# Twelve of 39 expert blocks transposed by DMA from 16-bit planes, in a fused linear and mixture-of-experts kernel

## The chip, the cores and the metric

The kernel runs on one core of one Trainium2 chip. The metric is device time in microseconds (us); lower is better. TensorE (PE) multiplies, ScalarE (ACT), VectorE (DVE) and GpSimd (POOL) do the elementwise work, SyncE (SP) issues most DMAs; POOL issues the indirect ones.

## The reference

2048 tokens of width 1024 pass a linear layer whose weight is masked in 32x32 blocks, and then a mixture of eight experts of which each token takes two:

```python
w_masked = weight * elem_mask
x = x + layernorm(x) @ w_masked.T            # x: 2048 x 1024
z = layernorm(x)
logits = z @ W_gate + b_gate
top_idx = top_k(logits, 2)
y_all = relu(z @ W_e[e] + b_e[e])            # e = 0..7, W_e[e]: 1024 x 1024
x = x + mean(y_all[top_idx])
```

All is fp32. A product is done as three passes of fp32r matmuls: high part by high part, high by low, low by high, so each operand is split into a rounded half (HI) and a rest (LO).

## The kernel before, in words

**Projection, about 0 to 220 us.** 16 token blocks of 128. For block t, PE multiplies x (xT) with the masked weight (wT) in two column halves of three passes of eight matmuls (`project_pass(t, n, pass)`). ACT first writes a row scaled by the block's mean into the PSUM half (`seed_mean(t, n)`, from t = 4 on; PE's first pass of a half waits for it through `c_sown`). `x_hi(t)` (ACT) and `x_lo(t)` (DVE) split the block's input; `mean1`, `square1` sum its rows; `residual`, `stats2` (DVE) and `inverse_std2` (POOL) give the second layer norm, and ACT's `norm2(t)` writes the normed rows into x2, a ring of two, from where SP stores them to DRAM (`store_x2`, tensor x2_rows). The gate's products go `gate(t)` (PE), `gate_out(t)` (ACT, copies them to gated), `logits(t)` (PE, waits for `gate_out(t)`). On PE the order around t = 4 is: pass (3,1,2), logits(0), gate(1), pass (4,0,0), logits(1), gate(2), passes (4,0,1) and (4,0,2), gate(3), logits(2), pass (4,1,0), gate(4). Up to t = 8 the order of each engine is written out by hand; a loop writes the rest. In the loop ACT also makes the HI half of the first expert's eight weight chunks (`HI0_AT`).

**Experts, about 220 to 690 us.** 39 blocks b of 128 rows, each of one expert. POOL gathers the block's rows by token number from x2_rows (`gather_rows`, ring of four buffers), PE transposes them (`transpose_rows`: eight 128x128 transposes against an identity, into PSUM) at the start of block b-1, ACT copies the result twice (`rows_hi`: xT HI, then x2T in fp32; both count in `c_rhi`), POOL subtracts to LO (`rows_lo`). PE then does two halves of 24 matmuls. ACT writes the bias into PSUM ahead of each half (`seed_half`), takes the relu of it into xb after it, and POOL adds xb to the output by an indirect DMA (`add_rows`). DVE splits the next expert's eight weight chunks (`split_chunk`) as soon as the expert that used the slot is through.

Every engine works in its own written order; semaphores tie them. An instruction that waits holds all behind it on its engine. ACT's order in block b is: rows of b+1, relu of half 0, bias of half 0 of b+1, relu of half 1, bias of half 1 of b+1.

Of the kernel before, what the change touches and what calls it, by code (L numbers as in the profile page):

```python
# [9 lines left out]
I32 = mybir.dt.int32  # L10
ALU = mybir.AluOpType
# [3 lines left out]
P = 128  # L15
# [7 lines left out]
def build(nc, data, weight, w_gate, b_gate, w_e, b_e, data_t, weight_t, mask_blocks, out):  # L23
# [26 lines left out]
    with ctx:  # L50

        x2_rows = nc.dram_tensor("x2_rows", (N_TOK, D), F32, kind="Internal").ap()

# [25 lines left out]

        raw = sb("raw", [P, 2, H], F32)  # L80
        bias_slot = sb("bias_slot", [P, 2, H], F32)
# [116 lines left out]
        through = sb("through", [P, N_EXP], I32)  # L198
        tok_half = sb("tok_half", [P, NH], I32)
        assert cursor[0] <= xr_offset + 2 * D * 4 and end <= nc.sbuf_usable_end  # L200

        def rows_of(b, cols=slice(0, D)):
            return (rows_a[:, cols], rows_b[:, cols], x2[:, 0, cols], x2[:, 1, cols])[b % 4]
# [90 lines left out]
        c_first, c_pick = sem("c_first"), sem("c_pick")  # L294
        c_tok_half = sem("c_tok_half")
# [4 lines left out]
        HI0_AT = {10: (0,), 11: (1, 2), 12: (3, 4), 13: (5, 6), 14: (7,)}  # L300
        GATHER_AT = NB - 2

# [18 lines left out]
        def _(eng):  # L321
# [71 lines left out]
            for t in (1, 2):  # L393
                store_x1(t)
                store_x2(t)
# [11 lines left out]
            for i in range(FIRST, NB + 1):  # L407
                if FIRST + 3 <= i + 1 < NB:
                    load_rows(i + 1)
                store_x1(i - 1)  # L410
# [9 lines left out]
                store_x2(i - 1)  # L420

            eng.wait_ge(s_spare, 16)
# [20 lines left out]
        def _(eng):  # L443
# [284 lines left out]
            def transpose_rows(b):  # L728
                eng.wait_ge(l_gather[b % 4], 16 * (b // 4 + 1))
# [68 lines left out]
            for b in range(EARLY, N_BLOCKS):  # L798
                if b > EARLY and b + 1 < N_BLOCKS:
# [3 lines left out]
                eng.wait_ge(c_rhi, 2 * b - 1)  # L803
# [15 lines left out]
        def _(eng):  # L819
# [75 lines left out]

            def norm2(t):
                if t >= 2:
                    eng.wait_ge(l_x2[t % 2], 16 * (t // 2))
                eng.wait_ge(c_rs2, RS2 * (t + 1))
# [27 lines left out]
            x_hi(2)  # L927
            mean1(1)
            square1(1)
            sum_diagonal(0)  # L930
            sum_diagonal(1)
            x_hi(3)
            sum_diagonal(2)
            sum_diagonal(3)
            sum_diagonal(4)
            mean1(2)
            square1(2)
            sum_diagonal(5)
            mean1(3)
# [774 lines left out]
```

## Time and profile before

| | us |
|---|---|
| median of 3 runs | 692.05 (690.92 to 694.01) |
| the profiled execution | 691.73 |
| its span | 689.5 |
| PE busy, share of the span | 671.3, 97% |
| DVE, ACT, POOL busy | 307.7, 289.5, 282.6 |
| granted TensorE clock, mean | 0.994 of full |

The span runs from the first to the last instruction on the engines. A busy PE is not PE at its peak: the ends of matmuls are modelled, and where instructions follow each other closely what counts is the distance between their starts. The expert stage is 39 blocks of about 11.8 us.

### The profile page before, as it was taken

The page shows a single profiled execution, that of the slowest core. Times are in us where ns is not written, and L with a number is a line of the kernel's source. Part 1 is how long each engine was busy: PE and PEld are TensorE (multiplying, and loading weights), DVE is VectorE, ACT ScalarE, POOL GpSimd, SP SyncE. Part 2 cuts the span into 40 slices and gives each one's busy share as a digit, 9 for nine tenths or more (in the row PEclk, how much of TensorE's full clock was granted, in tenths as well). Part 3 has the DMA queues.
Part 4 walks back from the last instruction along what each step waited for, and adds up shares of the span by engine and source line. Part 5 has one row for each costly group of instructions (what it writes and reads, how often), then busy time and mean ns, then how long its engine had stood idle before and what let it go on. Part 6 is the DMA issues. An engine that isn't in the chain of part 4 may idle for free.

```text
span 689.5 us, 11082 instructions
## 1 busy us (share of the span) xinstructions
PE 671.3 (97%) x3551; PEld 547.0 (79%) x3551; DVE 307.7 (45%) x551; ACT 289.5 (42%) x421; POOL 282.6 (41%) x253
## 2 busy tenths in 40 slices
PE   6999999999999999999999999999999999999993
PEld 5667777888887888888888888888888888888883
DVE  5886688877985562460642610551533420000000
ACT  7875544455743343333334343434333333434330
POOL 2023122135661365363635444463535363534331
PEclk9999999999999999999999999999999999999997
DMA  8992735497552579594784855694875854322223
GB/s 350 407 397 65 279 118 189 165 323 259 188 202 85 184 196 257 163 245 123 203 254 97 251 150 115 171 241 109 236 221 112 257 113 95 53 44 43 49 35 57
DMA packets 34900, 122.39 MB, mean 177 GB/s; under 512 B 5024, under 2 KB 5024, under 8 KB 34848
## 3 DMA queue, kind: packets, MB, share of 16 engines
q1 hardware_dynamic: 23472, 84.46, 33.7%
q0 software_dynamic: 11376, 37.23, 26.4%
q8 instruction: 33, 0.54, 0.3%
q14 instruction: 19, 0.16, 0.1%
HBM read 87.59 MB, written 37.75 MB: 182 GB/s over the span
## 4 chain that ended last, share of the span: by engine, by line
PE 96%; DMA 1%; ACT 1%; issue 0%; SPq 0%; POOLq 0%; DVE 0%; ACTq 0%
PE psO L449 83%; PE psT L739 5%; PE psT L449 2%; PE psT L482 2%; PE psO L482 1%; PE psG L555 1%; DMA xb<-data_t 1%; PE psS L536 1%; PE psT L523 0%; PE psT L567 0%; POOLq L50 0%; PE psT L544 0%; DVE w_stage L1318 0%; SPq L347 0%; ACT xT L829 0%
## 5 line engine op out<-in xcount | busy, mean ns | idle before, releaser
L449 PE MATMUL psO<-slots,xT 128*128 (+1 forms) x1872 | 435.9, 392 | 0.0
L449 PEld LDWEIGHTS psO<-slots,xT 128*128 128x128 f32 x1872 | 348.2, 188 | 70.6
L1056 ACT ACTIVATE xb<-psO 128x512 f32<-128x512 f32 x78 | 46.7, 599 | 254.5 <-PE psO L449 254.5
L449 PE MATMUL psO<-wT,xT 128*128 128x512 f32 x624 | 152.3, 397 | 0.8 <-ACT psO L887 0.8
L1645 POOL DMA_INDIRECT rows_out<-xb,tok_of x36 | 61.4, 1704 | 212.1 <-ACT xb L1056 211.8
L1306 DVE CAST slots<-raw 128x1024 fp32r<-128x1024 f32 x56 | 49.7, 887 | 191.0 <-PE psO L449 108.8
L449 PEld LDWEIGHTS psO<-wT,xT 128*128 128x128 f32 x624 | 114.3, 188 | 25.9 <-issue 2.7
L1639 POOL TENSOR_TENSOR xT<-x2T,xT 128x1024 fp32r<-128x1024 f32 x38 | 98.0, 2579 | 18.0 <-ACT x2T L1035 17.8
L1308 DVE TENSOR_TENSOR slots<-raw,slots 128x1024 fp32r<-128x1024 f32 x56 | 81.3, 1452 | 1.9
L996 ACT ACTIVATE psO<-bias_slot 128x512 f32 (+1 forms) x78 | 47.0, 602 | 35.6 <-ACT xb L1056 19.6
L1030 ACT ACTIVATE xT<-psT 128x1024 fp32r<-128x1024 f32 x38 | 38.4, 1011 | 7.5 <-PE psT L739 7.5
L1035 ACT ACTIVATE x2T<-psT 128x1024 f32<-128x1024 f32 x38 | 38.7, 1017 | 0.0
L1578 POOL TENSOR_SCALAR rs<-squares 128x1 f32<-128x1 f32 x16 | 9.5, 594 | 69.5 <-ACT rows_a L863 41.1
L1591 POOL TENSOR_SCALAR rs<-mv 128x1 f32<-128x1 f32 x16 | 5.2, 328 | 66.2 <-DVE mv L1097 66.1
L1604 POOL DMA_INDIRECT x<-x_rows,tok_of x19 | 25.5, 1344 | 6.1 <-DVE tok_of L1504 3.1
L829 ACT ACTIVATE xT<-xb 128x1024 fp32r<-128x1024 f32 x12 | 12.7, 1061 | 25.0 <-PE psO L449 19.4
L1631 POOL TENSOR_TENSOR slots<-w_stage,slots 128x1024 fp32r<-128x1024 f32 x8 | 19.2, 2416 | 9.5 <-ACT slots L1016 9.5
L739 PEld LDWEIGHTS psT<-ident,x 128*128 128x128 f32 x152 | 17.7, 140 | 2.5
L739 PE MATMUL psT<-ident,x 128*128 128x128 f32 x152 | 19.7, 272 | 0.0
L1165 DVE TENSOR_TENSOR row_hot<-lane,pos_r 128x1024 f16<-128x1024 f16 x16 | 19.5, 1217 | 0.0
L887 ACT ACTIVATE psO<-raw,minus_mean 128x512 f32<-128x512 f32 x24 | 16.3, 679 | 5.7 <-DVE xr L1110 4.3
L482 PE MATMUL psO<-wT,xT 128*128 128x512 f32 x48 | 13.5, 402 | 3.1 <-ACT wT L843 3.1
(227 smaller groups left out, 507.5 us busy)
## 6 DMA issues: line engine op xcount, KB each, us to landing
raw<-L_ffn_W_e SPq DMA_DIRECT2D x56, 512.0 KB, 5.1
x_rows<-x SPq DMA_DIRECT2D x16, 512.0 KB, 4.6
xb<-data_t SPq DMA_DIRECT2D x12, 512.0 KB, 4.3
mask_stage<-mask_blocks SPq DMA_DIRECT2D x8, 512.0 KB, 10.5
w_stage<-weight_t SPq DMA_DIRECT2D x8, 512.0 KB, 11.2
row_stage<-L_attn_weight SPq DMA_DIRECT2D x8, 512.0 KB, 12.2
xr<-L_attn_data SPq DMA_DIRECT2D x8, 512.0 KB, 5.7
rows_out<-xr SPq DMA_DIRECT2D x8, 512.0 KB, 3.0
```

The costliest lines, as they stand in the source:

```text
L449: last = eng.matmul(psum, xT[:, p, a, kt, :], moving(b, kt), start=(i == 0 and kt == 0 and not seeded), stop=(i == len(PASSES) - 1 and kt ...
L482: mm = eng.matmul(acc(t, n), xT[:, t, part_x, c, :], wT[:, part_w, c, n * HALF:(n + 1) * HALF], start=(i == 0 and c == 0), stop=(i == 1 an ...
L739: last = eng.transpose(psT[:, turn_bank(b), kt, :], rows_of(b, slice(kt * P, (kt + 1) * P)), ident[:])
L996: eng.activation(psO[:, n, :], bias, ACT.Copy).then_inc(c_seed, 1)
L1030: eng.activation(xT[:, b % 2, HI, :, :], psT[:, turn_bank(b), :, :], ACT.Copy).then_inc(c_rhi, 1)
L1035: eng.activation(x2T[:], psT[:, turn_bank(b), :, :], ACT.Copy).then_inc(c_rhi, 1)
L1056: eng.activation(xb[:, b % 2, n * HALF:(n + 1) * HALF], psO[:, n, :], ACT.Relu, scale=1.0 / TOP_K).then_inc(c_out, 1)
L1306: eng.tensor_copy(slots[:, e % 2, HI, kt, :], raw[:, kt % 2, :]).then_inc(c_split, 1)
L1308: eng.tensor_tensor(slots[:, e % 2, LO, kt, :], raw[:, kt % 2, :], slots[:, e % 2, HI, kt, :].bitcast(F32), ALU.subtract).then_inc(c_split, 1)
L1604: eng.indirect_dma_start(rows_of(b), None, x2_rows[0:known, :], bass.IndirectOffsetOnAxis(ap=tok_col(b), axis=0), bounds_check=known - 1, ...
L1639: eng.tensor_tensor(xT[:, b % 2, LO, :, :], x2T[:], xT[:, b % 2, HI, :, :].bitcast(F32), ALU.subtract).then_inc(c_rlo, 1)
L1645: eng.indirect_dma_start(out, bass.IndirectOffsetOnAxis(ap=tok_col(b), axis=0), xb[:, b % 2, :], None, bounds_check=N_TOK + P - 1, compute ...
```

## The change

Twelve blocks (b = 5, 8, 11, ..., 38) are no longer transposed by PE. For this the normed rows are also stored as two planes of 16-bit halves: ACT copies each 128x1024 fp32 block as 128x2048 16-bit values into `planes` (a single buffer, over raw[0]), SP stores it to a second DRAM tensor. For those twelve blocks POOL gathers plane rows into x2[1], a DMA issued by ACT transposes them into `turned`, and ACT joins the halves into x2T and rounds that to xT. The other blocks share three row buffers. In the written-out part of the projection ACT's order is new; one HI chunk of the first expert comes up to one iteration later; SP waits for the last planes store ahead of the second expert's weights, which land in the same buffer; and DVE's chunk splits for experts 2 to 7 are released in pairs, half a block apart, in place of all at once.

```diff
+        planes = at("planes", [P, 2, D], U16, raw_offset)
+        turned = at("turned", [P, 2 * KT, P], U16, xr_offset + D * 4)
         def rows_of(b, cols=slice(0, D)):
-            return (rows_a[:, cols], rows_b[:, cols], x2[:, 0, cols], x2[:, 1, cols])[b % 4]
+            ring = 3 if by_dma(b) else turns_of_pe(b) % 3
+            return (rows_a[:, cols], rows_b[:, cols], x2[:, 0, cols], x2[:, 1, cols])[ring]
-        HI0_AT = {10: (0,), 11: (1, 2), 12: (3, 4), 13: (5, 6), 14: (7,)}
+        HI0_AT = {10: (0,), 11: (1, 2), 12: (3,), 13: (4, 5), 14: (6,), 15: (7,)}
+        def by_dma(b):
+            return b > EARLY + 2 and b % 3 == 2
...
+            def store_planes(t):
+                eng.wait_ge(c_planes, t + 1)
+                eng.dma_start(x2_planes[t * P:(t + 1) * P, :], planes[:].rearrange("p h d -> p (h d)")).then_inc(l_planes, 16)
             store_x2(0)
             load_x(7)
-            for t in (1, 2):
-                store_x1(t)
-                store_x2(t)
+            store_planes(0)
+            store_x1(1)
+            store_x2(1)
+            store_planes(1)
+            store_x1(2)
+            store_x2(2)
...
+                store_planes(i - 2)
                 store_x1(i - 1)
...
-            eng.wait_ge(s_spare, 16)
+            eng.wait_ge(l_planes, 16 * NB)
...
-                if b > EARLY and b + 1 < N_BLOCKS:
+                if b > EARLY and b + 1 < N_BLOCKS and not by_dma(b + 1):
                     transpose_rows(b + 1)
-                eng.wait_ge(c_rhi, 2 * b - 1)
+                eng.wait_ge(c_rhi, 2 * b if by_dma(b) else 2 * b - 1)
...
+            def split_planes(t):
+                eng.wait_ge(c_ln2, t + 1)
+                if t == 0:
+                    eng.wait_ge(s_spare, 16)
+                else:
+                    eng.wait_ge(l_planes, 16 * t)
+                eng.activation(planes[:], x2[:, t % 2, :].bitcast(U16).rearrange("p (d h) -> p h d", h=2), ACT.Copy).then_inc(c_planes, 1)
...
+            norm2(0)
+            split_planes(0)
             gate_out(0)
-            norm2(0)
+            x_hi(5)
+            norm2(1)
             seed_mean(4, 0)
+            split_planes(1)
             gate_out(1)
-            x_hi(5)
             seed_mean(4, 1)
             gate_out(2)
...
+            def turn_rows(b):
+                eng.wait_ge(l_gather[3], 16 * turns_of_dma(b))
...
+                eng.dma_start_transpose(turned[:], rows_of(b).bitcast(U16)).then_inc(l_turn, 16)
+            def join_rows(b):
+                eng.wait_ge(l_turn, 16 * turns_of_dma(b))
+                eng.wait_ge(c_rlo, b - 1)
+                eng.activation(x2T[:].bitcast(U16).rearrange("p k (t h) -> p h (k t)", h=2),
+                               turned[:].rearrange("p (h k) t -> p h (k t)", h=2), ACT.Copy).then_inc(c_rhi, 1)
+                eng.wait_ge(c_rhi, 2 * b - 1)
+                eng.wait_ge(c_half, NH * b)
+                eng.activation(xT[:, b % 2, HI, :, :], x2T[:], ACT.Copy).then_inc(c_rhi, 1)
...
+                if b + 1 < N_BLOCKS and by_dma(b + 1):
+                    join_rows(b + 1)
...
+                    if n == NH - 1 and b + 3 < N_BLOCKS and by_dma(b + 3):
+                        turn_rows(b + 3)
...
             for e in range(2, N_EXP):
                 for kt in range(KT):
+                    if kt % 2 == 0:
+                        when = pace[0:1, kt // 2 - 1, e - 2:e - 1] if kt > 0 else through[0:1, e - 2:e - 1]
+                        used = eng.value_load(when, min_val=NH, max_val=NH * (N_BLOCKS + 1))
+                        eng.wait_ge(c_half, used)
                     split_chunk(e, kt)
...
+            eng.wait_ge(c_planes, NB)
+            eng.memset(x2[:, 1, :], 0.0).then_inc(c_clear, 1)
             add_rows(0)
             for b in range(1, N_BLOCKS):
-                if b + 1 < N_BLOCKS:
+                if b + 1 < N_BLOCKS and not by_dma(b + 1):
                     rows_lo(b + 1)
-                if b + 3 < N_BLOCKS:
+                if b + 3 < N_BLOCKS and not by_dma(b + 3):
                     gather_rows(b + 3)
+                if b + 4 < N_BLOCKS and by_dma(b + 4):
+                    gather_rows(b + 4)
+                if b + 1 < N_BLOCKS and by_dma(b + 1):
+                    rows_lo(b + 1)
```

**ACT in the written-out part of the projection, before.** From `square1(5)` on; psT,squares is `square1`, gated is `gate_out`, x2 is `norm2`, psO is `seed_mean`, xT is `x_hi`.

```order
L863 ACTIVATE psT,squares1_103<-xr_58,minus_mean1_102 128x1024
L894 ACTIVATE gated_82<-psG 128x128
L900 ACTIVATE x2_60<-w_stage_50,shift2_99,inverse2_98 128x1024
L887 ACTIVATE psO<-raw_55,minus_mean1_102 128x512
L894 ACTIVATE gated_82<-psG 128x128
L829 ACTIVATE xT_59<-w_stage_50 128x1024
L887 ACTIVATE psO<-raw_55,minus_mean1_102 128x512
```

**The same place on ACT, changed.** The new name planes is `split_planes`.

```order
L890 ACTIVATE psT,squares1_104<-xr_59,minus_mean1_103 128x1024
L936 ACTIVATE x2_61<-w_stage_50,shift2_100,inverse2_99 128x1024
L929 ACTIVATE planes_56<-x2_61 128x2048
L921 ACTIVATE gated_83<-psG 128x128
L856 ACTIVATE xT_60<-w_stage_50 128x1024
L936 ACTIVATE x2_61<-w_stage_50,shift2_100,inverse2_99 128x1024
L914 ACTIVATE psO<-raw_55,minus_mean1_103 128x512
L929 ACTIVATE planes_56<-x2_61 128x2048
L921 ACTIVATE gated_83<-psG 128x128
L914 ACTIVATE psO<-raw_55,minus_mean1_103 128x512
```

`x_hi(5)` and `norm2(1)` now stand ahead of `seed_mean(4, 0)`, and the planes copies of blocks 0 and 1 ahead of `gate_out(0)` and `gate_out(1)`.

**SP at the same time, before.** rows_out<-w_stage is `store_x1`, x_rows `store_x2`, xb<-data_t `load_x(7)`.

```order
L358 DMA rows_out<-w_stage 128x1024
L362 DMA x_rows<-x_60 128x1024
L332 DMA xb<-data_t 128x1024
L358 DMA rows_out<-w_stage 128x1024
L362 DMA x_rows<-x_60 128x1024
```

**The same place on SP, changed.**

```order
L376 DMA rows_out<-w_stage 128x1024
L380 DMA x_rows<-x_61 128x1024
L350 DMA xb<-data_t 128x1024
L384 DMA x_planes<-planes 128x2048
L376 DMA rows_out<-w_stage 128x1024
L380 DMA x_rows<-x_61 128x1024
L384 DMA x_planes<-planes 128x2048
```

The store of the planes of block 0 stands behind `load_x(7)`, and that of block 1 behind `store_x2(1)`.

**ACT in the expert stage, before, in one block.** xb<-psO is the relu, psO<-bias_slot the bias of the next block, xT and x2T are `rows_hi`.

```order
L1056 ACTIVATE xb_57<-psO 128x512
L996 ISA
L996 ACTIVATE psO<-bias_slot_56 128x512
L1030 ACTIVATE xT_59<-psT 128x1024
L1035 ACTIVATE x2T_61<-psT 128x1024
L1056 ACTIVATE xb_57<-psO 128x512
```

**ACT in the expert stage, changed: the end of block 2, and the rows of block 5 in block 4.** turned is the DMA's destination; the first piece stands behind block 2's last bias, the second ahead of block 4's first relu.

```order
L1123 ACTIVATE xb_58<-psO 128x512
L1039 ISA
L1039 ACTIVATE psO<-bias_slot_57 128x512
L1077 DMA_TRANSPOSE turned_165<-x2_61 128x16x128
L1095 ACTIVATE xT_60<-psT 128x1024
...
L1039 ACTIVATE psO<-bias_slot_57 128x512
L1082 ACTIVATE x2T_62<-turned_165 128x2x1024
L1086 ACTIVATE xT_60<-x2T_62 128x1024
L1123 ACTIVATE xb_58<-psO 128x512
```

The DMA for block b+3 is issued at the end of ACT's part of block b, one block and a piece ahead of the copy that reads it.

## Rows read from the trace of the kernel before

**Rows 1.** The page, part 4: the chain that ended last, by engine.

```profile
PE 96%; DMA 1%; ACT 1%; issue 0%; SPq 0%; POOLq 0%; DVE 0%; ACTq 0%
```

**Rows 2.** PE's waits, whole span: waited for, us in total, times, longest.

```profile
PE psO L449 <- ACT psO L887: 0.8, 1, 0.8
```

**Rows 3.** Timeline of PE, expert stage: start us, us, engine, line.

```profile
255.64 1.04 PE L739 MATMUL psT<-ident,rows_a 128*128 128x128 f32 x8
...
645.26 11.18 PE L449 MATMUL psO<-slots,xT 128*128 x48
656.28 1.03 PE L739 MATMUL psT<-ident,x 128*128 128x128 f32 x8
657.07 22.03 PE L449 MATMUL psO<-slots,xT 128*128 x96
```

**Rows 4.** Timeline of PE and ACT over one block, 409 to 428 us.

```profile
409.73 0.60 ACT L996 ACTIVATE psO<-bias_slot 128x512 f32 x1
...
421.40 11.16 PE L449 MATMUL psO<-slots,xT 128*128 x48
421.54 0.60 ACT L996 ACTIVATE psO<-bias_slot 128x512 f32 x1
...
427.21 0.60 ACT L1056 ACTIVATE xb<-psO 128x512 f32<-128x512 f32 x1 [3.21 <-PE psO L449]
```

**Rows 5.** The page, part 5: busy us, mean ns of one, idle before.

```profile
L996 ACT ACTIVATE psO<-bias_slot 128x512 f32 (+1 forms) x78 | 47.0, 602 | 35.6 <-ACT xb L1056 19.6
L829 ACT ACTIVATE xT<-xb 128x1024 fp32r<-128x1024 f32 x12 | 12.7, 1061 | 25.0 <-PE psO L449 19.4
```

**Rows 6.** DMA issues, 380 to 430 us: median us from issue to landing.

```profile
rows_out<-xb,tok_of POOLq DMA_INDIRECT x4, 6.4
x<-x_rows,tok_of POOLq DMA_INDIRECT x2, 4.8
```

**Rows 7.** Timeline of the written-out projection, 64 to 77 us.

```profile
64.48 2.12 PE L449 MATMUL psO<-wT,xT 128*128 128x512 f32 x8
64.79 1.23 ACT L900 ACTIVATE x<-w_stage,shift,inverse 128x1024 f32<-128x1024 f32 x1
65.78 0.27 POOL L1596 TENSOR_SCALAR shift<-mv,inverse 128x1 f32<-128x1 f32 x1
65.92 0.68 ACT L887 ACTIVATE psO<-raw,minus_mean 128x512 f32<-128x512 f32 x1
...
67.22 2.12 PE L449 MATMUL psO<-wT,xT 128*128 128x512 f32 x8
67.36 0.28 ACT L894 ACTIVATE gated<-psG 128x128 f32<-128x128 f32 x1 [0.76 <-PE psG L555]
67.40 0.33 SPq L332 DMA_DIRECT2D xb<-data_t  x1
...
69.18 0.29 PE L567 MATMUL psT<-diagonal,gated 128*128 128x16 f32 x2
...
76.68 0.64 PE L555 MATMUL psG<-w_stage,gates 128*32 128x128 f32 x16
```

**Rows 8.** DMA issues, 60 to 90 us: KB, median us to landing.

```profile
rows_out<-w_stage SPq DMA_DIRECT2D x4, 512.0 KB, 5.5
```

**Rows 9.** Line L362, the 16 stores of x2.

```profile
DMA to landing us min/median/max: 2.6/4.6/7.4
```

**Rows 10.** Timeline, 118 to 120 us: ACT's seed of block 8, PE's use.

```profile
118.47 0.67 ACT L887 ACTIVATE psO<-raw,minus_mean 128x512 f32<-128x512 f32 x1
119.70 5.71 PE L449 MATMUL psO<-wT,xT 128*128 128x512 f32 x24
```

**Rows 11.** One-us window behind PE's last matmul: busy times, then PEclk, DMA.

```profile
681.00:682.00 1.00, 0.00 (x0) 0.00 (x0) 0.00 (x0) 0.00 (x0) 0.63 (x1) 0.77 0.00 0
```

**Rows 12.** Timeline of DVE: end of one expert's splits, start of the next.

```profile
306.57 3.29 DVE L1308 TENSOR_TENSOR slots<-raw,slots 128x1024 fp32r<-128x1024 f32 x1
326.54 0.69 DVE L1306 CAST slots<-raw 128x1024 fp32r<-128x1024 f32 x1 [16.68 <-PE psO L449]
```

More of the change, by code:

```diff
@@ L10 @@
 I32 = mybir.dt.int32
+U16 = mybir.dt.uint16
 ALU = mybir.AluOpType
@@ L299, in build, with turns_of_pe, turns_of_dma @@
         FIRST_KNOWN, FIRST_TOK = 4, 15
-        HI0_AT = {10: (0,), 11: (1, 2), 12: (3, 4), 13: (5, 6), 14: (7,)}
+        HI0_AT = {10: (0,), 11: (1, 2), 12: (3,), 13: (4, 5), 14: (6,), 15: (7,)}
         GATHER_AT = NB - 2
+        def by_dma(b):
+            return b > EARLY + 2 and b % 3 == 2
+        def turns_of_pe(b):
+            return len([c for c in range(1, b + 1) if not by_dma(c)])
+        def turns_of_dma(b):
+            return len([c for c in range(1, b + 1) if by_dma(c)])
         def turn_bank(b):
@@ L949, in _ @@
             square1(5)
+            norm2(0)
+            split_planes(0)
             gate_out(0)
-            norm2(0)
+            x_hi(5)
+            norm2(1)
             seed_mean(4, 0)
+            split_planes(1)
             gate_out(1)
-            x_hi(5)
             seed_mean(4, 1)
             gate_out(2)
-            norm2(1)
-            mean1(6)
+            norm2(2)
+            split_planes(2)
+            norm2(3)
             gate_out(3)
             seed_mean(5, 0)
+            split_planes(3)
+            gate_out(4)
+            mean1(6)
+            x_hi(6)
             square1(6)
-            norm2(2)
-            gate_out(4)
-            norm2(3)
-            x_hi(6)
             seed_mean(5, 1)
             norm2(4)
+            split_planes(4)
             gate_out(5)
             seed_mean(6, 0)
+            mean1(7)
             x_hi(7)
+            square1(7)
             seed_mean(6, 1)
-            mean1(7)
-            square1(7)
             norm2(5)
+            split_planes(5)
+            seed_mean(7, 0)
             gate_out(6)
-            seed_mean(7, 0)
+            mean1(8)
+            square1(8)
             x_hi(8)
@@ L979, in _ @@
             norm2(6)
+            split_planes(6)
+            seed_mean(8, 0)
             gate_out(7)
-            mean1(8)
-            square1(8)
-            seed_mean(8, 0)
             def seed_half(b, slot, n):
@@ L1007, in _ @@
                 norm2(i - 1)
+                if i == NB:
+                    split_planes(i - 1)
                 if i < NB:
@@ L1049, in _ @@
             for b in range(N_BLOCKS):
-                if 1 < b + 1 < N_BLOCKS and b != 1:
+                if 1 < b + 1 < N_BLOCKS and b != 1 and not by_dma(b + 1):
                     rows_hi(b + 1)
+                if b + 1 < N_BLOCKS and by_dma(b + 1):
+                    join_rows(b + 1)
                 if b >= 2:
```

52 lines of the change are left out of this document (39 added, 13 removed).

## The prediction

> **What bounds the kernel now.** I read the chain that ended last first: 96% of it is PE [rows 1]. Then PE's waits: in the whole span, outside the first 30 us, PE stood once for ScalarE, 0.8 us [rows 2]. So nothing but PE's own stream sets the time: what is taken out of that stream is won, and what makes PE stand is lost in full, since no later slack takes it back. Third, the timeline of PE, for what a transposed block costs [rows 3]. Fourth, around every place where the change puts something ahead of an instruction that PE waits for, the timeline of that stretch, for how much room there is [rows 4, 7, 10, 12].
>
> **Part 1, the transposes that PE loses.** From the transposes at 255.64 to those at 656.28 are 34 blocks [rows 3], so 400.64 / 34 = 11.78 us for each with its eight transposes. The last block has none in front of it: the run of 96 matmuls takes 22.03 where one of 48 takes 11.18, so it adds 10.85 us [rows 3]. The difference, 0.93 us, is one price of eight transposes. The other is from their start to the next matmul, 657.07 - 656.28 = 0.79 us. I take the middle, 0.87. Twelve blocks lose them: 12 x 0.87 = 10.4 us (9.5 to 11.2). The same run of 96 shows that PE needs no pause to load the next block's slot number.
>
> **Part 2, do the twelve blocks come in time?** The DMA for block k is issued behind the last bias of block k-3, which is 409.73 + 0.60 = 410.3 in the rows [rows 4]. Block k-1 then starts at 421.40, and block k would at 421.40 + 10.85 = 432.3. Between landing and that start ACT has to do the join, the rounding copy, one relu and one bias. The join is 2048 elements of 16 bits; no row shows such a copy. 512 elements take 0.60 and 1024 take 1.06 us [rows 5], so 0.46 for each 512 and, if 16 bits go at the rate of 32, 1.06 + 2 x 0.46 = 1.98. Bounds: 1.06 (twice the rate) and 4.0 (half the rate). I take 1.98, the nearest to the rows. 1.98 + 1.06 + 0.60 + 0.60 = 4.2, so the rows have to land by 428.1, 17.8 us behind the issue. The transposing DMA is not in the trace either. It moves 512 KB; its nearest rows are the gather of the same size, 4.8 us, the add, 6.4 us [rows 6], and the slowest of sixteen 512 KB stores, 7.4 us [rows 9]. Lower bound 2.6 [rows 9]; as upper bound I take four times the gather, 19.2, since the values are moved in pieces of 16 bits. I take about 7 us. All but the top of this range is hidden by the block in between: cost 0. Joined before the relu at 427.21 [rows 4], it even leaves ACT's order as it was. ACT's own work grows by about 1 us in a block where it stood 3.2 us before the relu alone [rows 4].
>
> The Trainium skill speaks on this with two voices. "VectorE: DVE Perf Modes", section "The three transpose paths", gives 1309 ns for one 128x128 square of 16 bits by DMA. A block is 16 such squares, one after the other 20.9 us, and by that rule the deadline would be missed by 3 us each time. "Advanced Engine Details and Errata", section "X-Bar Transpose (TRN2)", has such DMAs as fast as ordinary ones, which would leave 10 us and more. No row of before decides it.
>
> **Part 3, the new ACT order in the projection.** Here PE has no reserve. Before, `seed_mean(4, 0)` ran at 65.92 and PE began pass (4,0,0) at 67.22 [rows 7]. Now `x_hi(5)` stands ahead of it, which waits until projection 3 is done, 64.48 + 2.12 = 66.60 [rows 7]. Then `x_hi` 1.06 [rows 5], `norm2(1)` 1.23 (its shift is there at 66.05) and the seed 0.68 [rows 7]: 69.6. PE stands from 67.2 to 69.5: **2.3 us**.
>
> Next on PE is logits(1), 1.96 us behind the pass (67.22 to 69.18) [rows 7], so at 71.5. It needs `gate_out(1)`, and that stands behind `split_planes(1)`, which needs the single planes buffer, so the landing of block 0's planes. SP issues that store behind `load_x(7)` at 67.40 + 0.33 [rows 7], so at 67.75. The stores of that stretch take 5.5 us [rows 8] (2.6 to 7.4 [rows 9]): 73.25. Planes copy 1.98, `gate_out` 0.28: 75.5. PE stands from 71.5 to 75.5: **4.0 us** (1.2 to 6.0 by the landing's bounds).
>
> The pattern returns once: `split_planes(2)` waits for the store of block 1's planes, issued at 75.3, and `norm2(3)` and `gate_out(3)` stand behind it: 75.3 + 4.6 + 1.98 + 1.23 + 0.28 = 83.4. PE wants gate(4) at 7.5 us behind logits(1) (69.18 to 76.68 [rows 7]), 83.0: **0.3 us** with some room for error. Sum 6.6 us (3.5 to 9.5).
>
> Further on the planes copy takes the place of the mean and square of block 8 ahead of `seed_mean(8, 0)`, which ends 0.6 us before PE wants it [rows 10]; it takes no longer than the two instructions of 1024 elements that it replaces, at 1.06 each [rows 5]. In the loop it stands behind the next block's first seed, ahead of nothing that PE wants within half a block. Cost 0, as long as the copy takes 2 us.
>
> **Part 4, the rest.** 16 more stores of 512 KB, the gathers at the same number, the cleared buffer, and SP's wait for the last planes (one store more, about 5 us) all end before their users: expert 1 is needed only after the first expert's blocks. The paced splits cannot end later than about 18 us plus two chunks behind the release; now the splits of an expert end 16.7 us before the next release [rows 12]. Cost 0, hidden by that gap.
>
> **The sum.** -10.4 + 6.6 = -3.8 us in the profiled execution, 691.73 to 687.9; its time is 0.3 below the median of the runs shown, so 692.05 - 3.8 = **688.2**. Half a percent, 3.5 us, is what a measurement of this kernel can tell from no change, so the forecast lies on the edge of faster.
>
> **Rivals.**
> A. The projection's stalls stay small, because the planes' store lands in 2.6 us or ScalarE's waits resolve sooner: loss 0 to 3.5, time 681.6 to 685.1. For it: the fastest of the stores took 2.6 [rows 9]. Against it: the first stall, 2.3 us, hangs on no DMA.
> B. The clock falls in the gap of 4 us. After PE's last matmul (657.07 + 22.03 = 679.1) the granted clock is 0.77 in the microsecond from 681 on [rows 11], so 2 to 3 us of a standing PE at 2.4 GHz end at 1.2 GHz. For it: the gap is longer than that. Against: a row for a gap inside running work is missing. Matmuls at half rate for 2 to 4 us more than now cost 1 to 4 us: 689 to 692.
> C. The other side: the transposed rows land late. PE then stands before each of the twelve blocks, and ACT, which waits in the join, holds the relu and the bias too. It decides from 17.8 us on, and each further us costs 12. At 19.2 us, the upper bound above: 12 x 1.4 = 17 us, 705. For it: 16-bit pieces, beside gathers and adds that fill the queues in bursts; against it: no 512 KB transfer in rows 6, 8 and 9 takes half as long. By the page's 20.9 us it would be 12 x 3.1 = 37 us, 725.
> D. The planes copy runs at half the rate, 4.0 us. Then +2.0 on the second stall, +2.1 on the third place (77.3 + 4.6 + 4.0 + 1.23 + 0.28 = 87.4 against 77.5 + 7.5), about 1.3 at `seed_mean(8, 0)` (2.0 more against 0.6 of room, rows 10): 688.2 + 5.4 = 693.6.
> E. The change does not do what it says: the transposes go, but PE's stream does not close up behind them. The run of 96 matmuls speaks against it [rows 3]; I give it no share of its own.
>
> **How the numbers follow.** Forecast 42% (own range 685 to 691; 27 of it faster by over 0.5%, 15 within), A 15% (faster), B 15% (within), D 12% (half within, half slower, if other waits add to it), C 16% (slower, in any form, ACT's time to issue the DMA included). Faster 0.42, within 0.36, slower 0.22. The range from 681.8 to 700 leaves out the far end of C and the best of A.
>
> **What would show it.** In the profile after: no transposes of PE before blocks 5, 8, ..., 38, and block periods of 10.9 us there against 11.8; PE idle for `seed_mean` near 67 us (2.3), for `gate_out` near 71.5 (4.0); a planes copy of about 2 us; a transposing DMA that lands within 10 us; no idle time of PE after 240 us. Wrong would be: PE waits on x2T or a bias in the expert stage (C), no gap before 85 us (A), a clock below 1.0 between 72 and 85 us (B).

## The result, and the profile after

| | before | after |
|---|---|---|
| median, us | 691.53 (690.84 to 694.01, 22 runs) | 696.97 (691.45 to 708.29, 22 runs) |
| the profiled execution | 691.73 | 701.13 |
| its span | 689.5 | 699.4 |
| granted TensorE clock, mean | 0.994 | 0.980 |

The ratio of after to before is 1.0055, 95% interval 1.0034 to 1.0077: slower, where I forecast 688.2, half a percent faster. (It leaves out executions that count as disturbed and so lies nearer to 1 than the ratio of the medians.) The single times of after are of two kinds: nine lie within 691.4 to 693.8, the other thirteen spread from 696 to 708. Before has none above 694.1.

PE's waits of after, from 60 us on; columns as in [rows 2], where one line stood:

```profile
PE psT L594 <- ACT gated L921: 4.7, 1, 4.7
PE psO L476 <- ACT psO L914: 3.1, 2, 2.3
...
PE psT L766 <- DMA rows_b<-x_rows,tok_of: 2.9, 1, 2.9
PE psO L476 <- ACT psO L1039: 2.8, 1, 2.8
...
PE psT L550 <- DVE blk_tok L1237: 0.5, 1, 0.5
```

And the chain that ended last, where PE had 96% [rows 1]:

```profile
PE 89%; DMA 6%; ACT 1%; issue 1%; DVE 1%; SPq 0%; ACTq 0%; POOLq 0%; DVEq 0%
```

The DMA's share by line is turned 3%, x_planes 1% and xb (data_t) 1%: two of the three are the change's. The timeline of the written-out projection of after, the same pieces as [rows 7]:

```profile
67.25 1.06 ACT L856 ACTIVATE xT<-w_stage 128x1024 fp32r<-128x1024 f32 x1 [1.79 <-PE psO L476]
...
68.22 1.23 ACT L936 ACTIVATE x<-w_stage,shift,inverse 128x1024 f32<-128x1024 f32 x1
68.34 1.18 SPq L384 DMA_DIRECT2D x_planes<-planes  x1
...
69.35 0.67 ACT L914 ACTIVATE psO<-raw,minus_mean 128x512 f32<-128x512 f32 x1
...
70.17 3.16 PE L476 MATMUL psO<-wT,xT 128*128 128x512 f32 x8 [2.31 <-ACT psO L914]
...
75.94 1.91 ACT L929 ACTIVATE planes<-x 128x2048 uint16<-128x2048 uint16 x1 [5.92 <-DMA x_planes<-planes]
...
78.07 0.61 PE L594 MATMUL psT<-diagonal,gated 128*128 128x16 f32 x2 [4.74 <-ACT gated L921]
```

Both stalls are where the forecast had them: 2.31 us before the pass, then ACT waits for the landing of block 0's planes (issued at 68.34, landed 7.5 us later, in time for 75.94) and PE for the gate behind it. But the pass itself took 3.16 us where it took 2.12. PE in windows of after (busy, count, granted clock, DMA share, GB/s):

```profile
66.00:68.00 2.00, 1.86 (x24) 1.00 0.93 193
68.00:70.00 2.00, 0.00 (x0) 1.00 0.96 389
70.00:72.00 2.00, 1.83 (x6) 0.72 0.97 389
72.00:78.00 6.00, 1.33 (x4) 0.50 0.71 289
78.00:84.00 6.00, 5.93 (x28) 0.50 0.67 267
84.00:86.00 2.00, 2.00 (x15) 0.87 1.01 406
86.00:90.00 4.00, 4.00 (x46) 1.00 0.46 183
```

PE stood from 67.9 to 70.2, and behind that the granted clock fell to 0.50, the 1.2 GHz level, and was back at 1.00 from 86 us on. Busy time times what the clock lacked, window by window: 1.83 x 0.28 + 1.33 x 0.5 + 5.93 x 0.5 + 2.00 x 0.13 = 4.4 us lost on top of the stalls as they were measured.

The same can be read from starts alone, of after against before. Pass (4,0,0) begins 70.17 - 65.04 = 5.13 us after pass (3,1,2), against 67.22 - 64.48 = 2.74: 2.4 more. From there to logits(1) it is 78.07 - 70.17 = 7.90 against 1.96: 5.9 more. From logits(1) to gate(4), where PE waits for nothing, it is 10.54 (gate(4) begins at 88.61) against 7.50: 3.0 more. That makes 11.4 us, as does 2.3 + 4.7 + 4.4. But it shows what the low clock costs by itself, 3.0 us: the rest of the 4.4 fell into pass (4,0,0), and without it PE would only have stood that much longer for the same landing.

In the expert stage the gain is there. PE of after, to be read against [rows 3]:

```profile
609.80 11.15 PE L476 MATMUL psO<-slots,xT 128*128 x48
...
621.58 22.04 PE L476 MATMUL psO<-slots,xT 128*128 x96
...
644.25 11.18 PE L476 MATMUL psO<-slots,xT 128*128 x48
655.26 1.03 PE L766 MATMUL psT<-ident,x 128*128 128x128 f32 x8
```

A block with transposes takes 621.58 - 609.80 = 11.78 us, two with one set 644.25 - 621.58 = 22.67; one without is 10.89, a gain of 0.89. But once in the profiled execution the transposed rows came late. The same engines as in [rows 4], from the issue on:

```profile
406.87 22.03 PE L476 MATMUL psO<-slots,xT 128*128 x96
...
407.08 1.34 ACTq L1077 DMA_TRANSPOSE turned<-x  x1
407.15 0.33 SPq L429 DMA_DIRECT2D bias_slot<-L_ffn_b_e  x1
407.77 1.57 POOL L1729 DMA_INDIRECT rows_out<-xb,tok_of  x1 [7.19 <-ACT xb L1123]
...
413.11 1.43 POOL L1688 DMA_INDIRECT rows_b<-x_rows,tok_of  x1 [0.17 <-issue]
...
429.66 2.49 ACT L1082 ACTIVATE x2T<-turned 128x2048 uint16<-128x2048 uint16 x1 [10.27 <-DMA turned<-x]
430.00 1.57 POOL L1729 DMA_INDIRECT rows_out<-xb,tok_of  x1 [15.46 <-DMA rows_out<-xb,tok_of]
431.79 1.17 PE L766 MATMUL psT<-ident,rows_b 128*128 128x128 f32 x8 [2.88 <-DMA rows_b<-x_rows,tok_of]
...
435.74 12.94 PE L476 MATMUL psO<-slots,xT 128*128 x48 [2.79 <-ACT psO L1039]
...
448.52 1.03 PE L766 MATMUL psT<-ident,x 128*128 128x128 f32 x8
```

The transpose landed 22.6 us after its issue, and it was not alone: an add issued 0.7 us behind it held POOL's next add for 15.46 us, and a gather issued at 413.11, 4.8 us in [rows 6], let PE go on 18.7 us later. By the periods above, PE's transposes of 448.52 were due at 406.87 + 22.67 + (655.26 - 644.25) = 440.55: 8.0 us lost, of which 5.7 are PE's two waits. Most of the other 2.3 is the low clock again: it was 0.50 between 434 and 438 us, and the 48 matmuls of 435.74 took 12.94 us, not 11.18. The other eleven joins waited for nothing.

The profiled execution adds up: -12 x 0.89 + 2.3 + 4.7 + 4.4 + 8.0 = +8.7 us; measured +9.4, and +9.9 between the spans. Of the 1.2 us left of the latter, 0.56 were there before the first stall (pass (3,1,2) begins at 65.04 against 64.48), and 0.5 is PE's wait for DVE's blk_tok, which before doesn't have.

### The profile page after: what moved, and what is told of

Its sections match the earlier page's. It is cut to its first block, busy times and chain, and to the rows that moved or that the text cites. A ratio compares the mean times of both kernels' runs of the same rounds, so it can differ in the third digit from the quotient of the medians.

```text
span 699.4 us, 11039 instructions
## 1 busy us (share of the span) xinstructions
PE 667.6 (95%) x3455; PEld 541.2 (77%) x3455; DVE 305.2 (44%) x554; ACT 339.0 (48%) x437; POOL 280.9 (40%) x254
## 4 chain that ended last, share of the span: by engine, by line
PE 89%; DMA 6%; ACT 1%; issue 1%; DVE 1%; SPq 0%; ACTq 0%; POOLq 0%; DVEq 0%
PE psO L476 78%; DMA turned<-x 3%; PE psT L766 3%; PE psT L509 2%; PE psT L476 2%; PE psO L509 1%; PE psG L582 1%; DMA xb<-data_t 1%; DMA x_planes<-planes 1%; PE psS L563 1%; PE psT L550 0%; PE psT L594 0%; ACT x2T L1082 0%; DVE pos_r L1250 0%; ACT xT L856 0%
## 5 line engine op out<-in xcount | busy, mean ns | idle before, releaser
L476 PE MATMUL psO<-wT,xT 128*128 128x512 f32 x624 | 155.6, 403 | 3.1 <-ACT psO L914 3.1
L1729 POOL DMA_INDIRECT rows_out<-xb,tok_of x36 | 66.1, 1837 | 189.3 <-ACT xb L1123 160.4
L1375 DVE CAST slots<-raw 128x1024 fp32r<-128x1024 f32 x56 | 53.0, 946 | 192.9 <-PE psO L476 107.7
L1723 POOL TENSOR_TENSOR xT<-x2T,xT 128x1024 fp32r<-128x1024 f32 x38 | 94.5, 2487 | 36.8 <-ACT x2T L1100 34.5
L1377 DVE TENSOR_TENSOR slots<-raw,slots 128x1024 fp32r<-128x1024 f32 x56 | 75.5, 1348 | 1.9
L1095 ACT ACTIVATE xT<-psT 128x1024 fp32r<-128x1024 f32 x26 | 26.5, 1020 | 27.0 <-issue 21.3
L1082 ACT ACTIVATE x2T<-turned 128x2048 uint16<-128x2048 uint16 x12 | 30.2, 2516 | 10.3 <-DMA turned<-x 10.3
L929 ACT ACTIVATE planes<-x 128x2048 uint16<-128x2048 uint16 x16 | 30.4, 1903 | 6.1 <-DMA x_planes<-planes 5.9
L1100 ACT ACTIVATE x2T<-psT 128x1024 f32<-128x1024 f32 x26 | 26.5, 1018 | 0.0
L936 ACT ACTIVATE x<-xr,shift,inverse 128x1024 f32<-128x1024 f32 x8 | 9.9, 1243 | 14.9 <-POOL shift L1670 14.9
L856 ACT ACTIVATE xT<-xb 128x1024 fp32r<-128x1024 f32 x12 | 12.7, 1059 | 8.5 <-PE psO L476 5.9
L509 PE MATMUL psO<-wT,xT 128*128 128x512 f32 x48 | 13.5, 402 | 3.4 <-ACT wT L870 3.4
## 6 DMA issues: line engine op xcount, KB each, us to landing
mask_stage<-mask_blocks SPq DMA_DIRECT2D x8, 512.0 KB, 11.3
row_stage<-L_attn_weight SPq DMA_DIRECT2D x8, 512.0 KB, 11.4
```

Source lines behind the costliest of these rows:

```text
L476: last = eng.matmul(psum, xT[:, p, a, kt, :], moving(b, kt), start=(i == 0 and kt == 0 and not seeded), stop=(i == len(PASSES) - 1 and kt ...
L509: mm = eng.matmul(acc(t, n), xT[:, t, part_x, c, :], wT[:, part_w, c, n * HALF:(n + 1) * HALF], start=(i == 0 and c == 0), stop=(i == 1 an ...
L929: eng.activation(planes[:], x2[:, t % 2, :].bitcast(U16).rearrange("p (d h) -> p h d", h=2), ACT.Copy).then_inc(c_planes, 1)
L1082: eng.activation(x2T[:].bitcast(U16).rearrange("p k (t h) -> p h (k t)", h=2), turned[:].rearrange("p (h k) t -> p h (k t)", h=2), ACT.Cop ...
L1095: eng.activation(xT[:, b % 2, HI, :, :], psT[:, turn_bank(b), :, :], ACT.Copy).then_inc(c_rhi, 1)
L1100: eng.activation(x2T[:], psT[:, turn_bank(b), :, :], ACT.Copy).then_inc(c_rhi, 1)
```

## The experiments

All are edits of the changed kernel and are compared with before, which had medians of 691.33 to 691.61 in the five sets.

### The projection

**planes_only**: no block goes by DMA; everything else of the change stays.

```diff
-            return b > EARLY + 2 and b % 3 == 2
+            return False
```

> The planes are copied, stored and waited for as in the changed kernel, with its ACT order, but PE transposes all 39 blocks and no transposing DMA is issued. Theory 1 (the projection loses about 12 us: 2.3 and 4.7 us of standing PE, about 4 us at 1.2 GHz, 1 us small): 691.5 + 12 = 703 to 704, with little scatter between runs. Theory 2 (the time goes mostly to DMA jams of the transposes, and to the copies of ACT in the expert stage): 697 or less.

Measured: 702.91 us (700.68 to 705.13), ratio 1.0145 (1.0123 to 1.0168). The preparation alone costs 11.3 us.

**act_order**: the same instructions, in an order where no seed or gate stands behind a planes store that has just gone out.

```diff
+            seed_mean(4, 0)
             x_hi(5)
-            norm2(1)
-            seed_mean(4, 0)
-            split_planes(1)
             gate_out(1)
             seed_mean(4, 1)
+            norm2(1)
             gate_out(2)
+            mean1(6)
+            split_planes(1)
+            gate_out(3)
...
```

(and so on: each planes copy behind the seed and the gate next due.)

> The changed kernel, with the written-out part of ACT's order rewritten: seed_mean(4,0), x_hi(5) and gate_out(1) ahead of norm2(1), and each planes copy behind the instruction that PE waits for. Theory 1: no gap on PE before 85 us, no fall of the clock, 691.5 - 10.4 = 681 in a run without a jam, and the slow runs above that stay. Theory 2: under 3 us better than the changed kernel.

Measured: 681.86 us (681.40 to 696.13), ratio 0.9851 (0.9831 to 0.9871). PE's waits from 60 us on, and 60 to 90 us in one window:

```profile
PE psO L476 <- ACT psO L914: 0.8, 1, 0.8
```

```profile
60.00:90.00 30.00, 30.00 (x226) 1.00 0.68 262
```

Both stalls and the low clock are gone, with every copy and store still made. So it was the order alone that cost 10 us. One of its six runs, 696.13, shows that the late landings have another cause.

**seed_first**: only the first stall taken back.

```diff
+            seed_mean(4, 0)
             x_hi(5)
             norm2(1)
-            seed_mean(4, 0)
             split_planes(1)
```

> The changed kernel with one instruction moved: the seed of block 4's first half stands ahead of the rounding copy of block 5 and the norm of block 1 again. My sum gave the first stall 2.3 us, the trace showed 2.3. Theory S1, the two stalls are in series and the second ends with the landing of the planes store: removing the first alone wins little, since PE only arrives earlier at logits(1), which still waits to the same end; the standing time moves there (gap 4.7 becomes about 7), time minus 0 to 1. Rival S2, they add: time minus 2.3, the gap at the gate stays 4.7. Read from the gaps in the profile, because the median is blurred by the late transposes (691.5 to 708).

Measured: 696.49 us (691.16 to 706.84), ratio 1.0038 (1.0011 to 1.0066). PE's waits:

```profile
PE psT L594 <- ACT gated L921: 7.8, 1, 7.8
...
PE psO L476 <- ACT psO L914: 0.8, 1, 0.8
```

The first stall of 2.3 is gone (the 0.8 is another wait, near 225 us, which before has too), and the second has grown from 4.7 to 7.8: PE comes earlier to logits(1) and waits there for the same landing. logits(1) begins 12.7 us behind pass (3,1,2), against 13.0 in after.

**fill_gap** and **fill_both** put matmuls whose results nobody reads where PE would stand; fill_both has more of them, and issues the transposes half a block earlier.

```diff
+            warm(20)                 # fill_both: warm(34)
             project_pass(4, 0, 0)
+            warm(44)                 # fill_both: warm(70)
             logits(1)
```

> The changed kernel with 20 and 44 small matmuls that nothing reads, put on PE into the two gaps, ahead of pass (4,0,0) and of logits(1). Both waits stay. If the clock falls because PE stands, it stays at 2.4 GHz now, and 3 to 4 us come back: fastest runs at 687.5 to 689 against 691.5 of the changed kernel. If the clock has another cause, the time is the same or up to 1 us longer.

> turn_half_earlier with both gaps of the projection filled with small matmuls that nothing reads (34 and 70). The waits stay. If the low clock is the consequence of the standing PE, it vanishes before 600 us, and the median falls from 691.9 by 3 to 4 us to about 688. If it is not, no change.

Measured: fill_gap 691.44 us (687.71 to 700.93), ratio 0.9977 (0.9960 to 0.9995); PE still stood 3.4 us and the clock fell behind that, so its time told little. fill_both 688.82 us (688.24 to 690.39), ratio 0.9960 (0.9947 to 0.9973), against 691.87 for turn_half_earlier below, the same kernel without the fill. Windows of turn_half_earlier and of fill_both:

```profile
66.00:90.00 24.00, 18.42 (x117) 0.79 0.79 301
```

```profile
66.00:90.00 24.00, 23.30 (x235) 1.00 0.80 308
```

The data PE waits for come no sooner (logits(1) begins at 76.62 without the fill and at 76.77 with it); what comes back, 3.0 us, is the clock. From logits(1) to gate(4) it is 10.60 us without the fill and 7.59 with it, 3.0 again. The clock's share is lost because PE stands: the DMA traffic of the stretch is nearly the same in both (301 and 308 GB/s).

### The room of the transposes

**turn_half_earlier**: the transposing DMA goes out behind the first half's bias, some 5.5 us sooner.

```diff
-                    if n == NH - 1 and b + 3 < N_BLOCKS and by_dma(b + 3):
+                    if n == 0 and b + 3 < N_BLOCKS and by_dma(b + 3):
```

> The changed kernel with the transposing DMA issued half a block earlier, behind the bias of half 0 and not of half 1, so about 6 us ahead of the add and of the next weights rather than beside them. If the slow runs come from these meeting the transposing DMA, or from too short a lead, they get rarer: median near 692. If they come from elsewhere (the gathers, the three buffers), the scatter from 691 to 706 stays.

Measured: 691.87 us (690.94 to 694.07, 12 runs), ratio 1.0002 (0.9989 to 1.0015). Nothing lies above 694.1 any more. Against planes_only this gives the steady gain of the twelve transposes: 702.91 - 691.87 = 11.0 us, 0.92 each.

**turn_half_later**: behind the first half's bias of the next block, some 6 us later.

```diff
-                    if n == NH - 1 and b + 3 < N_BLOCKS and by_dma(b + 3):
-                        turn_rows(b + 3)
+                    if n == 0 and b + 2 < N_BLOCKS and by_dma(b + 2):
+                        turn_rows(b + 2)
```

> The changed kernel with the transposing DMA issued half a block later than it has it, behind the bias of half 0 of the next block: the lead over the join shrinks from 12 to about 6 us, but the DMA no longer starts beside the add and the next weights. Theory 'phase' (jams come from what is in flight when it starts): no jams, 691 to 694, unless a landing of over 6 us makes PE stand a little. Theory 'lead' (jams only matter because the lead is short): clearly worse than the changed kernel, median over 700.

Measured: 718.63 us (708.75 to 730.03), ratio 1.0315 (1.0279 to 1.0351). PE's waits and the landings of the twelve:

```profile
PE psO L476 <- ACT psO L1039: 25.6, 4, 10.0
```

```profile
DMA to landing us min/median/max: 4.3/7.6/20.5
```

So theory "lead" came true: with less room ACT waited for eight of the twelve landings (50.7 us in all). And away from the add there are late landings still, of 16.1, 18.0 and 20.5 us.

**order_and_half**: act_order and turn_half_earlier together.

> Both repairs in one: ACT's rewritten order of act_order and the transposing DMA half a block earlier. Projection repaired (-11) and no jams: 681 to 682 in every run, scatter under 3 us. If the earlier issue only hid the jams by chance, one run in two or three lies at 690 or above.

Measured: 681.84 us (681.45 to 688.11), ratio 0.9860 (0.9846 to 0.9874). The profiled run is the one of 688.11, and here is why:

```profile
391.47 1.38 ACTq L1077 DMA_TRANSPOSE turned<-x  x1
...
392.97 0.57 SPq L429 DMA_DIRECT2D bias_slot<-L_ffn_b_e  x1
...
416.68 2.49 ACT L1082 ACTIVATE x2T<-turned 128x2048 uint16<-128x2048 uint16 x1 [8.89 <-DMA turned<-x]
```

So more room does not stop the late landings (25.2 us here, against my expectation), it takes most of their price: one run of five is longer, by 6.3 us.

### What makes a landing late

In the profiles the nine landings of 18 us or more share a neighbour: a 512 KB bias load issued within 2 us of the transpose. Between 15 and 18 us it is not so: the 15.8 of act_order and the 17.6 of one_row_bias have it, four others don't (17.5 and 15.7 in fill_both, 16.1 in turn_half_later, 17.3 in every_second_bias_mid). The first of these, issued at 536.94, had weight chunks beside it that took 15.8; at its earlier place it cost PE nothing. Nor does a bias load near by always do it: in after the transpose of 518.41 had one 1.4 us ahead, and nothing waited for it.

**one_row_bias** shrinks the bias loads of experts 2 to 7 to one row of 4 KB on one partition and leaves out the other 127, **one_row_loads** does so with their weight chunks as well.

```diff
+                if place >= 2:
+                    eng.dma_start(bias_slot[0:1, place % 2, :], b_e[bass.ds(expert, 1), :]).then_inc(l_bias[place % 2], 16)
+                    return
                 eng.dma_start(bias_slot[:, place % 2, :],
```

> The changed kernel, but the bias of experts 2 to 7 is loaded as one row on one partition (4 KB) and no longer copied to all 128 partitions (512 KB); the output of those experts has a wrong bias. In the profiled runs a transpose that took 18 to 25 us to land was issued within 2 us of such a bias load. Theory J1, that meeting makes the long landing: no transpose takes over 13 us, all runs lie near 691.5 (spread under 2 us), median 691 to 692. Rival J2, the long landing comes from weights, gathers and adds together, or from nothing that the kernel loads: some runs stay at 696 or more, longest landing 18 us or more.

> The changed kernel, but both the weights (8 chunks of 512 KB per expert) and the bias of experts 2 to 7 are loaded as single rows of 4 KB; their outputs are wrong. Theory J1 or J2 with the weights: no transpose over 13 us, all runs within 2 us of 691.5. Rival J3, the long landing has nothing to do with the loads but with the gathers and adds of rows: runs at 696 and more stay. If one_row_bias keeps them and this one doesn't, it is the weight chunks.

Measured: one_row_bias 692.82 us (690.01 to 702.09, 12 runs), ratio 1.0014 (0.9995 to 1.0034); one_row_loads 692.67 us (689.97 to 701.95, 11 runs), ratio 1.0015 (0.9993 to 1.0037). Neither bears out J1 as written: times above 694.5 stay. Fewer, though: above 694.5 are 5 of 12 and 2 of 11, against 13 of 22. The profile of one_row_loads shows where one is left, at block 5 beside the loads of expert 1, which I had left whole:

```profile
267.29 1.56 ACTq L1083 DMA_TRANSPOSE turned<-x  x1
268.33 0.41 SPq L432 DMA_DIRECT2D bias_slot<-L_ffn_b_e  x1
...
292.80 2.49 ACT L1088 ACTIVATE x2T<-turned 128x2048 uint16<-128x2048 uint16 x1 [13.21 <-DMA turned<-x]
```

In the profile of one_row_bias it is block 5 too: transpose at 267.48, bias at 269.48, landing after 17.6 us. So block 5 had to be taken out, with a control. **from_block_8** does that; **from_8_one_row_bias** and **from_8_one_row_loads** add the shrunk loads.

```diff
-            return b > EARLY + 2 and b % 3 == 2
+            return b > EARLY + 3 and b % 3 == 2
```

> The changed kernel, but block 5 is transposed by TensorE, so eleven blocks go by DMA. Control for the next two: block 5's transpose was the one that met expert 1's loads, which one_row_bias and one_row_loads left whole. By the sum one transpose less costs 0.9 us (undisturbed runs at 692.4). Theory J1 (a late landing comes where a transposing DMA, a 512 KB bias load and an add are issued within 2 us): later transposes still meet a bias, so runs above 696 stay, fewer than in the changed kernel (13 of its 22 lay above 695.9). Rival J4 (only block 5's transpose is ever disturbed): no run above 694.

> from_block_8, and the bias of experts 2 to 7 as one row of 4 KB (their output has a wrong bias). J1: nothing of that kind is left, no landing over 13 us, every run within 691 to 694.5, median 692.4. Rival J2 (weight chunks do it as well as the bias): runs above 696 stay.

> from_block_8, with bias and weight chunks of experts 2 to 7 as single rows of 4 KB (their outputs are wrong). J1 and J2: every run within 691 to 694.5, landings 4 to 8 us. Rival J3 (gathers and adds of rows alone make the late landing): runs above 696 stay.

| | median, us | runs | above 694.5 | ratio |
|---|---|---|---|---|
| from_block_8 | 700.03 (691.90 to 713.50) | 12 | 8 | 1.0058 (1.0025 to 1.0090) |
| from_8_one_row_bias | 693.01 (691.63 to 693.65) | 11 | 0 | 1.0022 (1.0013 to 1.0031) |
| from_8_one_row_loads | 692.86 (691.76 to 694.38) | 9 | 0 | 1.0027 (1.0017 to 1.0037) |

With 8 of 12 in the control, none in 11 is no accident: if the two were alike, such a split would come about once in a thousand. It is the full bias load that brings the late landings of that place in the block; weight chunks, gathers and adds were all still there in from_8_one_row_bias, and so was a one-row bias 1.4 us ahead of the transpose of 510.34. The control's profile has its late landing at 510 us, with the bias 0.14 us behind the transpose:

```profile
510.15 7.56 ACTq L1077 DMA_TRANSPOSE turned<-x  x1
510.29 0.33 SPq L429 DMA_DIRECT2D bias_slot<-L_ffn_b_e  x1
...
510.84 2.45 POOL L1729 DMA_INDIRECT rows_out<-xb,tok_of  x1 [7.45 <-ACT xb L1123]
```

Here even the issue took 7.56 us, in which ACT's queue stood.

**no_pace** and **early_no_pace** release an expert's splits, and so its loads, all at once; the second also has the earlier transposes.

```diff
-                    if kt % 2 == 0:
+                    if kt == 0:
```

> The changed kernel with the splits of an expert's weights released all at once, as before the change. Since DVE's splits release the loads of the next chunks, the loads then come closer together. Theory P1, pacing costs and brings nothing: median 691 to 702 with the same spread of runs as the changed kernel (691.5 to 708). Rival P2, pacing is what keeps the transposes undisturbed: more long landings, median above 703, PE waits in the expert stage over 12 us. Rival P3, pacing itself makes the meeting of loads and transpose: no run above 694.

> The changed kernel with the transpose issued half a block earlier and the splits of an expert released all at once. Turned half a block earlier with pacing it took 691.9 with no run above 694.1; without pacing and at the old place 703.5. Theory L (what matters is the room of the transposes, pacing only lowers the number and size of late landings): the 5.5 us more of room take in most landings, median 692 to 697. Rival M (pacing alone is what keeps landings short): median above 699.

Measured: no_pace 703.48 us (692.01 to 718.79, 13 runs, 12 of them above 697), ratio 1.0076 (1.0051 to 1.0100). early_no_pace 691.62 us (689.92 to 692.98, 11 runs), ratio 1.0004 (0.9995 to 1.0013). At the transposes' old place pacing is worth about 6 us, with 13 of 22 runs above 694.5 against 12 of 13; with 5.5 us more room it is worth nothing.

**bias_mid_block**, complete again: the bias goes out behind an expert's sixth weight chunk.

```diff
                     eng.dma_start(raw[:, kt % 2, :], w_rows(expert, kt)).then_inc(l_raw[kt % 2], 16)
-                load_bias(place, expert)
+                    if kt == 5 and place >= 2:
+                        load_bias(place, expert)
+                if place < 2:
+                    load_bias(place, expert)
```

> The changed kernel, complete, with the bias load of experts 2 to 7 behind the sixth of an expert's eight weight chunks instead of behind the last. Chunk loads are released in pairs half a block apart, so the bias now goes out in the middle of a block, where neither a transposing DMA nor an add is issued. Theory J1 (bias load, transpose and add issued within 2 us make the late landing): runs above 694 come at most from block 5 and expert 1, whose bias stays where it was (in the seven-odd profiles seen, 2 of 7 disturbed landings there); median 691.5 to 693. Rival J5 (a 512 KB bias load in flight anywhere near a transpose does it, whatever the phase): median 696 or more, as in the changed kernel.

Measured: 692.19 us (690.42 to 710.03), ratio 1.0026 (1.0001 to 1.0051); 4 of 12 above 696. The median is J1's, those four runs are not. It doesn't decide between J1 and J5, since for expert 2 the bias did not come out in mid-block: in the profile it went out at 303.50 us, 1.18 us behind the transpose of 302.32, and a later one 1.74 us behind that of 543.56. They landed after 12.0 and 4.7 us, so this profile has no late landing to look at.

### A version that beats both

**every_second**: order_and_half with 17 blocks by DMA.

```diff
-            return b > EARLY + 2 and b % 3 == 2
+            return b > EARLY + 2 and b % 2 == 1
-                    eng.wait_ge(c_rhi, 2 * (b - 3))
+                    eng.wait_ge(c_rhi, 2 * (b - 2))
```

> order_and_half with every second block from 5 on (17 instead of 12) transposed by DMA. If the gain is 0.92 us a block and nothing new waits, 681.5 - 5 x 0.92 = 677. If the single row buffer, the single turned buffer or the DMA queues are at their end, PE stands for a join and the time is 682 or more, with jams.

Measured: 676.62 us (676.28 to 677.29), ratio 0.9789 (0.9776 to 0.9802). Five transposes less give 5.2 us, 4.6 expected. The landings, none waited for:

```profile
DMA to landing us min/median/max: 4.3/5.5/11.3
```

**every_second_bias_mid** adds the bias move.

> The best kernel so far (norms by the repaired ScalarE order, every second block by DMA, issued half a block earlier: 676.6, 676.3 to 677.3) with the same move of the bias. There no landing was late enough to be waited for (longest 11.3 us). Expected the same: 676.6, within 676.0 to 677.5; below 676 would mean that the bias load still cost something there, above 677.5 that its new place meets the earlier transposes.

Measured: 676.83 us (676.57 to 677.17), ratio 0.9789 (0.9777 to 0.9802): the same. But its profile has a landing of 17.3 us, for which ACT's join stood 0.3 us and PE not at all. I ran each five times; a late landing that comes once in ten runs could still be in them.

## Why the prediction was wrong

**Part 1** was right: 10.4 us forecast (9.5 to 11.2), 11.0 by planes_only against turn_half_earlier, 10.7 by the periods. The stream closed up (rival E is out).

**Part 3** found the places and the waits; the sizes came near, and one price was missing. First stall 2.3, measured 2.31. Second 4.0, measured 4.74: the store took 7.5 us, not 5.5, just above the 7.4 of my bounds, and part of the longer wait was taken up by a pass at the low clock (by the starts it is 5.9 us). The third, 0.3, did not show. The planes copy takes 1.90 us where I took 1.98, so rival D is out. What the sum left out is rival B: the clock fell, at 1.2 GHz for about 14 us, and cost 3.0 us, by the starts and by fill_both alike (4.4 by the windows, but 1.2 of that lie in the pass ahead of the second wait). I had it as an alternative worth 15%, although its mechanism does not compete with the stalls but follows from them. A cost that follows from a term of the forecast belongs in the sum.

**Part 2** holds the step that failed and cost most: "All but the top of this range is hidden by the block in between: cost 0." The landing I took, about 7 us, is the usual one (median 5.5 in the profile of every_second, and never below 4.3). The deadline of 17.8 us was right too: at 22.6 it was missed. But I worked with one value for all twelve, and rival C with the same lateness twelve times. In the profiles with the transpose at this place none to two of them land late, the worst beside a bias load and in up to 25.8 us, while the rest land as usual. That moves the median from about 692 to 697. I gave the bias load no row and no thought, though the forecast was about where a 512 KB DMA is set among others. The join, 2.52 us against 1.98, cost nothing.

Without a late landing the change is thus worth -11.0 + 2.3 + 4.7 + 4.4 = +0.4 us, 691.9; the middle of the nine undisturbed runs of after is 692.3. The late landings are the other 4.7 us of the median. Of the 8.8 us by which the forecast missed, Part 2 thus has 4.7 and Part 3 the rest: 3.0 for the clock and 1.7 for longer stalls, less 0.6 that Part 1 gained; this adds up to within half a microsecond. Either one takes up the gain of 3.8 that I forecast. That 697 lies within my range of 681.8 to 700 is no merit of the working: its upper end stood for twelve moderately late landings, not for one very late one.

The two voices of the Trainium skill can now be heard against the runs. The figure in the Trainium skill's "VectorE: DVE Perf Modes", section "The three transpose paths", would be 20.9 us for sixteen squares one after the other, by my estimate; most landings take 4.3 to 8 us, so it can't be added up square by square (whether squares overlap or most of the figure comes once per DMA, no run shows). The late ones don't bear it out either, since at their old place they vanish with the bias load. The Trainium skill's "Advanced Engine Details and Errata", section "X-Bar Transpose (TRN2)", as fast as ordinary DMAs, agrees with the undisturbed landings (4.3 against the gather's 4.8) and says nothing of a bias load at the same time.

**Left open**: the four landings of 15 to 18 us without a bias load within 2 us; whether the phase of the bias load or only its size matters (bias_mid_block), and why one execution has the late landing and the next doesn't. Inside the bias load it was not tried what does it; it is the only load of the expert stage that copies one row of DRAM to all 128 partitions, and the only one that mattered at this place.

## What to carry to other kernels

Before new work goes into an engine's queue, ask of each instruction behind it when it is due; here the order alone was worth 10 us, twice what the whole change cost. When a stall of PE is forecast that is as long as those here (2.3 us and more), add the matmuls at half clock that follow it. Give a transposing DMA the room of its worst landing, not of its usual one, or keep it from being issued beside a broadcast load; and look at the spread of the runs, since a median can hide two kinds of execution.

## What the runs showed of the hardware

- A standing PE of 2.3 us brought the granted clock from 1.00 to 0.50, which then outlasted PE's return by some 6 us of nearly full work (78 to 84 us, busy 5.93 of 6). In before, where PE did not stand between 60 and 90 us, it was 1.00 there. A wait of 1.1 us in fill_gap did not lower it: it stayed at 1.00 until 76 us, in the wait of 3.4. In turn_half_earlier it had fallen to 0.50 by 70 to 72 us, was back at 1.00 in 74 to 76 us, while PE stood, and at 0.50 again from 78 us on, while PE worked.
- A transposing DMA of 128 rows of 4 KB lands in 4.3 us at best and 25.8 us at worst (no_pace), and its issue holds ACT's queue for 1.3 to 4.6 us in after, 7.6 us once in from_block_8.
- When it lands late other DMAs do too: in after an add and a gather, in fill_both weight chunks (15.8 us). Queues of after between 416 and 419 us, with 66 GB/s in all (q1 are SP's plain DMAs, q0 POOL's indirect ones, q10 the transposes; then packets, MB, and the time of the packets as a share of 16 engines):

```profile
q1 hardware_dynamic: 23, 0.09, 107.8%
q0 software_dynamic: 23, 0.09, 81.9%
q10 hardware_dynamic: 72, 0.02, 29.3%
```

  The DMA engines are shown as busy, but move a third of their mean of 196 GB/s.
- ACT copies 2048 16-bit elements in 1.90 us where the source is strided, and in 2.52 where the destination is (planes L929, join L1082):

```profile
L1082 ACT ACTIVATE x2T<-turned 128x2048 uint16<-128x2048 uint16 x12 | 30.2, 2516 | 10.3 <-DMA turned<-x 10.3
L929 ACT ACTIVATE planes<-x 128x2048 uint16<-128x2048 uint16 x16 | 30.4, 1903 | 6.1 <-DMA x_planes<-planes 5.9
```
